# Edge loop of a graph block: GpSimd issues the gathers of two halves on ahead of the multiply of the present half

## What is computed

```python
s0 = x0[sender]
s1 = x1[sender]
p1 = w1 * s0 * y0
p2 = (w2 * s0)[:, :, None] * y1[:, None, :]
p3 = w3[:, :, None] * s1 * y0[:, None, :]
p4 = w4 * jnp.einsum('eum,em->eu', s1, y1) / SQRT3
msg0 = jax.ops.segment_sum(m0, receiver, num_segments=num_nodes)
msg1 = jax.ops.segment_sum(m1, receiver, num_segments=num_nodes)
```

## Time and profile before

| | us |
|---|---|
| median of 3 runs | 2267.75 (2266.25 to 2269.3) |
| the profiled execution, its time | 2266.87 |
| its span in the trace | 2264.9 |
| end of the first block of the edge loop, from the span's start | 249.2 |
| end of its last block but one | 835.3 |
| end of its last block | 855.3 |

### The profile page before, as it was taken

How to read it: one execution, slowest core, us unless ns; L and a number is a source line. 1 busy time by engine, 2 the same in 40 slices (tenths; PEclk the granted TensorE clock), 3 DMA queues, 4 the chain that set the end, 5 groups by cost and what they waited for, 6 DMA issues and landing times.

```text
span 2264.9 us, 45107 instructions
## 1 busy us (share of the span) xinstructions
PE 2060.1 (91%) x13564; PEld 1487.3 (66%) x13565; DVE 1335.5 (59%) x2849; ACT 1040.0 (46%) x2316; POOL 618.2 (27%) x739
## 2 busy tenths in 40 slices
PE   7899888888888888799999999999599999889998
PEld 4444344344434337588888888888388888768886
DVE  3212788889888876655555555555612346664444
ACT  6531333333333332277777777777143223354443
POOL 2102677778777774300000000002100000000000
PEclk9999999999999998699999999999799999989999
DMA  6642566667676678355603420042700200310000
GB/s 217 220 164 85 151 188 186 188 185 191 187 190 190 181 210 317 136 194 197 260 19 117 156 79 19 19 167 85 260 10 10 84 19 19 107 43 10 10 10 18
DMA packets 157291, 288.52 MB, mean 127 GB/s; under 512 B 43533, under 2 KB 85270, under 8 KB 152615
## 3 DMA queue, kind: packets, MB, share of 16 engines
q1 hardware_dynamic: 111349, 158.80, 20.4%
q0 software_dynamic: 37552, 121.91, 18.7%
q10 hardware_dynamic: 8322, 6.89, 0.9%
HBM read 233.69 MB, written 53.85 MB: 127 GB/s over the span
## 4 chain that ended last, share of the span: by engine, by line
PE 60%; DVE 13%; issue 10%; DMA 9%; POOL 3%; ACT 3%; DVEq 1%; POOLq 1%; ACTq 0%; SPq 0%
PE psum L2548 14%; DMA big_b<-sender_table,wide 7%; PE psum L2686 6%; PE psum L2719 4%; PE psum L2538 4%; PE psum L2539 3%; PE psum L2540 3%; PE psum L2584 3%; PE psum L2593 3%; PE psum L2624 3%; PE psum L2614 2%; POOL big_b L1041 2%; DVE big_b L1721 2%; DVE big_b L1722 2%; PE psum L2266 2%
## 5 line engine op out<-in xcount | busy, mean ns | idle before, releaser
L1041 POOL DMA_INDIRECT big_b<-sender_table,wide x360 | 368.5, 1024 | 117.0 <-issue 84.2
L2397 PEld LDWEIGHTS psum<-big_b,wide 128*32 128x32 f32 x3600 | 166.2, 109 | 195.9 <-issue 134.3
L2367 PE MATMUL psum<-w_mlp,wide 64*128 64x512 f32 x728 | 206.9, 645 | 81.4 <-DVE big_b L1722 78.2
L2548 PEld LDWEIGHTS psum<-xn_T,big_b 128*128 128x128 f32 x2048 | 261.9, 191 | 21.1 <-issue 3.1
L2397 PE MATMUL psum<-big_b,wide 128*32 128x256 f32 (+2 forms) x3600 | 272.0, 390 | 0.8 <-POOL wide L1071 0.8
L2548 PE MATMUL psum<-xn_T,big_b 128*128 128x128 f32 x2048 | 265.0, 275 | 0.0
L1250 ACT ACTIVATE wide<-psum 128x384 f32<-128x384 f32 x45 | 22.1, 490 | 393.3 <-PE psum L2408 369.0
L1896 DVE TENSOR_TENSOR w_lo<-wide,w_hi 128x512 fp32r<-128x512 f32 x184 | 127.4, 692 | 117.9 <-ACT w_hi L1342 117.9
L2538 PE MATMUL psum<-w_hi,hid_hi 128*128 128x512 f32 x368 | 175.8, 478 | 9.5 <-DVE w_lo L1896 7.2
L1243 ACT ACTIVATE wide<-wide 128x290 bf16<-128x290 f32 x360 | 158.6, 527 | 41.9 <-PEq L2370 37.2
L1720 DVE TENSOR_TENSOR big_b<-psum,big_b 128x512 f32<-128x512 f32 x180 | 124.0, 689 | 84.8 <-DMA big_b<-sender_table,wide 70.6
(11 more groups left out here) (453 smaller groups left out, 3949.8 us busy)
## 6 DMA issues: line engine op xcount, KB each, us to landing
big_a<-in_L_ffn_W SPq DMA_DIRECT2D x12, 2048.0 KB, 13.9
big_b<-in_L_ffn_W SPq DMA_DIRECT2D x12, 2048.0 KB, 13.7
wide<-in_L_ffn_W SPq DMA_DIRECT2D x8, 2048.0 KB, 23.5
wide<-edge_hidden SPq DMA_DIRECT2D x182, 64.0 KB
edge_hidden<-wide SPq DMA_DIRECT2D x21, 512.0 KB, 3.1
tokens_sorted<-zeros SPq DMA_DIRECT2D x29, 256.0 KB
adj_dram<-big_a SPq DMA_DIRECT2D x1, 6400.0 KB, 23.5
xn_T<-tokens_sorted POOLq DMA_DIRECT2D x25, 256.0 KB, 2.9
```

What stands on the lines that cost most here:

```text
L1041: nc.gpsimd.indirect_dma_start(out=sent[q][:, j, :], out_offset=None, in_=sender_table, in_offset=bass.IndirectOffsetOnAxis(ap=indices[j], ...
L2367: last = nc.tensor.matmul(tile_w[q % 2][:, j, :], h3_slot[q][halves[j], :], w_mlp4[halves[j], :], start=True, stop=True)
L2397: nc.tensor.matmul(msg_psum[k].rearrange("p (c u) -> p c u", u=MUL)[bands[g], cols, :], hot_y[q][:, j, y, :], p[:, of, :], start=False, st ...
L2548: last = nc.tensor.matmul(psum[:, f % UP_BANKS, 0:P], ew1[a][:, c, f * P:f * P + P], tile_T[:, c, :], start=(c == 0), stop=(c == C - 1))
```

## The change

In every slot of the loop on POOL the two gathers for half q+2 and their waits now stand ahead of the multiply of half q and its waits; before, they stood behind it. Nothing is added or removed, and no other engine's program changes.

```diff
                     for q in range(HALVES):
                         ahead = (q + 2) % HALVES
+                        pool.wait_ge(record_loaded[ahead], s * 16 + (q + 2) // HALVES * 16)
+                        pool.wait_ge(products_done, s * 4 + q + 3)
+                        pool.sem_inc(loop_entered, 1)
+                        gather(ahead, record_senders(ahead))
                         pool.wait_ge(hot_low_ready, s * 4 + q + 5)
                         pool.wait_ge(scatter_done, s * 4 + q + 1)
                         pool.sem_inc(loop_entered, 1)
                         nc.gpsimd.tensor_tensor(hot_y[q], hot[q].unsqueeze(2).to_broadcast([P, 2, Y, GRAIN]),
                                                 record[q][:, :, 0:Y].unsqueeze(3).to_broadcast([P, 2, Y, GRAIN]), ALU.mult)\
                             .then_inc(hot_y_ready, 1)
-                        pool.wait_ge(record_loaded[ahead], s * 16 + (q + 2) // HALVES * 16)
-                        pool.wait_ge(products_done, s * 4 + q + 3)
-                        pool.sem_inc(loop_entered, 1)
-                        gather(ahead, record_senders(ahead))
```

## The result

| | before | changed |
|---|---|---|
| median, us | 2267.0 (4 runs, 2261.2 to 2269.3) | 2324.84 (4 runs, 2316.49 to 2331.43) |
| ratio, 95% interval | | 1.0258 (1.0239 to 1.0277) |
| the profiled execution, time and span, us | 2266.87, 2264.9 | 2331.43, 2329.6 |
| mean granted clock over the span | 0.972 | 0.959 |

The changed kernel is 2.6% slower, by 58 us. The forecast was slower too, by 29 us. The sign and the mechanism hold and the size is half, and the median lies 3 us above the range.

What follows compares the result with a forecast made beforehand. A block-long cycle through the late record and POOL's queued multiplies was to bound the loop: 14.31 us a block against 13.63, 43 x 0.68 = 29 us on 2267.75, so 2297 us; 8-in-10 range 2269 to 2322.

Steps and rivals of the forecast that it cites:

- late record: Next block's half 0 record, loaded by L843 only after the block's end and hot_step; its gather on POOL waits for it.
- the cycle through the multiply of half 3: Late record, gather, multiply of half 3, block end, next late record: 11.17 us in the old order, 14.31 after the change.
- Links 1 to 4: Block end to hot_step 1.86 us, to L843 0.32, record load to gather 4.06, gather to end of multiply 3 6.12.
- X: Issue of the late record's load to the start of its gather: 4.06 us, with 3.33 and 4.81 as ends.
- the heavier rival: X grows to 4.81 us always: 15.06 us a block, 2329 us; chance 0.11.
- The faster rival: Record there in time, earlier gathers pay: at the limit POOL's 12.56 us a block, 2222 us; chance 0.11.
- Link 5: End of multiply 3 to PE's start 0.10 us, then PE from L2397 to the end of L2408 1.85 us.
- The ends: First block may gain up to 2.4 us, last a few; set against block variation at 0, 3 us doubt.

Runs made afterwards that it cites:

- The slots on chip E: Gathers ahead of the multiply in some slots only, against the kernel before: slots 0 and 1 0.9985, slot 2 1.0054, slot 3 1.0162, slots 2 and 3 1.0246.
- the moved copy: PSUM copies L1250 and L1252 issued behind the next block's hot_steps in the kernel before: 0.9916 on chip D, 0.9846 on chip F; in the changed kernel 1.0071.
- The filler run: Changed kernel plus eight matmuls of zeros in PE's wait at half 2, against the kernel before on chip D: 1.0145, 2298.80 us.

## Why the prediction was half right

**The bound and the lever.** That each block has a late record, that its load waits for the block's end through hot_step, and that the old order has over 2 us to spare in the cycle through the multiply of half 3, all held. The slots on chip E show it: a link of 3.1 or 3.6 us leaves the block at 13.5, one of 5.7 or 6.3 makes it 13.9 to 14.2. The cycle is not the only one: with slot 2 early the one through the multiply of half 2 and PE's own 5.0 us rules, and the late record costs something in the old order too, as the moved copy showed.

**Links 1 to 4.** 1.86, 0.32, 4.06 and 6.12 us were forecast, and 2.12 (the first two together), 4.05 and 6.20 measured in the blocks at full clock. X did not grow there, so the heavier rival is out as a mechanism, though its time of 2329 us is nearest to the result. X did not shrink either. By the row of the late load and that of its gather, X was 3.92 and 3.94 us in the two blocks shown, and with the 0.86 us between the record's semaphore and the gather, 3.1 of it are the load itself. The faster rival fell with that. The Trainium skill (DMA: Bandwidth & Descriptors, "Anatomy of one DMA") has about 2.0 us as the fixed cost of a DMA. The trace doesn't agree for this load, 3.1 us here; but that section's fit is for DMAs issued from GpSimd, and the record load is issued by SP, which the prediction passed over. Nor is 3.1 us a fixed number: with slots 0 and 1 early on chip B the median of the record loads is 1.7 us from issue to landing, and X 2.8.

**Link 5, the step that failed.** It was priced at 1.95 us with the remark that the clock is at its full level throughout. That was read from the kernel before, where 1.00 is a rounded mean over a stretch with one low stretch in it, and the change itself took it away: PE waits 1.95 us on average for the multiply of half 2 in the blocks at full clock and 2.58 in the 18 of 42 with a low stretch, and in those the link is 3.29 us. That is 18 x 1.26 = 23 us in this link and, with the other links of these blocks, 34 in all, where the forecast had nothing. The filler run settles it: 2298.8 us with one low stretch, 2321.6 with 13. I had forecast the waits and not asked what the clock does behind them.

**What the forecast left out.** The second cycle, of 14.07 us, is only just shorter than the first, 14.40, and so hardly moved the result, but it would have told that a quicker block end alone can't save the new order.

**DVE.** Its wait for the gathers was to vanish because each gather is issued sooner against its own multiply. In halves 2 and 3 it fell, from 45 us to 26 between 290 and 840 us. In halves 0 and 1 it rose from 13 to 73. The gathers of these are issued when the late record is there, whatever stands behind them, and on a longer block DVE stands longer for them. A DVE wait for a DMA told how long the DMA's issue was held up, not that issuing it earlier in POOL's order would help.

**The ends.** The last block gave back 5.3 us, more than the 3 us of doubt that the forecast allowed (DVE's wait of the earlier trace rows was 5.89); the first block gained nothing that shows (248.9 instead of 249.2).

## What to carry to other kernels

Before an instruction is moved ahead of another on an engine that issues in order, write down the cycles that run through it (buffer released, load, wait, work, buffer released) with all the work of that engine between the wait and the release, and one for each instruction behind the wait that another engine needs. Compare each with the present period: the distance is what the move may cost free of charge. If the new bound makes TensorE wait two microseconds at a time, ask what the clock does behind the wait, and price the work there at the lower level as a case of its own; here it fell in 18 of 42 blocks. A few idle matmuls in the wait can be worth more than they cost, as they were on one kind of chip here. An experiment on slots or halves is to be read on the same chip as its reference, and once more on another.

## What was not expected of the hardware

- Nineteen low stretches, one of 6.83 us and the others of 3.41, in a loop where PE is busy 83% of the time. The length of PE's wait alone doesn't tell which block gets one: in the blocks with a low stretch PE's longest wait was 1.69 to 4.36 us, in those without it was up to 3.05.
- The same program takes 2265 to 2267 us on three chips and 2300 to 2306 on three others, and in the two traces compared the difference is in the edge loop alone. In the kernel before, ACT's copy starts up to 2.9 us behind the record of the matmul that releases it on chip C, of the slower kind, and at most 0.14 on chip A. One reordering costs 3.5 to 3.9% on the one kind and nothing on the other.
